# Tile order, shared rounds and filler products in the causal attentions of a four-layer decoder kernel

## Chip, core and metric

The kernel runs on one core of a Trainium2 chip. The metric is the time of one execution on the device in microseconds (us). The engines are TensorE (PE in the rows, its weight loads PEld), VectorE (DVE), ScalarE (ACT), GpSimd (POOL) and SyncE (SP, which issues the transfers).

## What is computed

A decoder of four layers works on x of shape (4, 512, 128). Each layer has an attention, a cross attention and a feed-forward part, each added to x behind a layer norm:

```python
x = x + _L0_attn_ref(_layernorm(x, axis=-1), ...)
x = x + _L0_xattn_ref(_layernorm(x, axis=-1), ctx_1024, ctx_1024, ...)
x = x + _L0_ffn_ref(_layernorm(x, axis=-1), ...)
...
x = x + _L3_ffn_ref(_layernorm(x, axis=-1), ...)
```

Three of the twelve parts are touched. The attention of layer 0 is a gated delta rule with 16 value heads over chunks: for each chunk a lower triangular matrix is inverted by doubling, and a state is carried from chunk to chunk; its output is gated by silu(x W_z). The feed-forward part of layer 0 is a mixture of 16 experts with 4 chosen. The attentions of layers 1 and 2 are causal softmax attentions over 512 positions with 16 heads: scores q k, masked above the diagonal, softmax over the keys, times v.

## The kernel before

The batch of four is a loop of four passes. A pass runs the twelve parts one after the other, each a block of its own in which every engine has its own program and semaphores order them; engines meet at a block's ends. All matrices lie as 128 partitions times 512 positions; NT = 4 tiles of 128 positions.

`causal_attention` serves both causal attentions, so it runs eight times in an execution. The heads are in G = 4 groups of R = 4; a group's four heads sit in the four 32-row strips of TensorE. PSUM has eight banks of 512 columns. Its work comes in two stages.

The score stage finds each query's peak. TensorE walks through `steps`. A step `("scores", g, i)` makes the scores of query tile i of group g against keys 0 to (i + 1) * 128 (four products, L624, and four small ones, L627, which add the mask on the diagonal) into one half of PSUM, banks 0 to 3 or 4 to 7 in turn. VectorE reduces each to the negated maximum (L705). When all tiles of a group are there, VectorE splits the peaks into a coarse and a fine part (L711 to L716). A step `("turn", g, 0)` transposes these (L633) into the half whose turn it is, and ScalarE copies them to `shiftT` (L679). Step n starts when the content of step n - 2, in the same half, is read.

The second stage makes the probabilities by key tile. A unit u is one key tile j of one group. TensorE computes k q for keys j and queries j * 128 to 512 and adds the negated peaks with a two-row product (`shifted`, L646 and L649, banks 0 to 3). ScalarE takes the exponential of all of it (L685) into one of three slots of `prob`, GpSimd zeroes what is above the diagonal (L695), and TensorE multiplies by v and by ones (`mix`, L663), two units later. VectorE takes the reciprocal of the sums and multiplies (L722, L724), after each group in layer 1 and once in layer 2 (`shared`). TensorE's program is shifted(u), then mix(u - 2), and shifted(u) waits for the exponential u - 1.

In `stage_l0_attn` a step n inverts the matrices of four pairs p in L = 6 levels. Each level has a half level (L2208, in the last level L2204), a copy by ScalarE (L2330), and a whole level (L2223 and L2227, in the last level L2218), and VectorE subtracts (L2498, in levels 5 and 6 L2502 and L2505). Between them TensorE places products of the step before (`ks` L2151, `corrected` L2168, `output` L2177, `add` L2187) and of the step to come (`prep` L2118 and L2122, `turn` L2130), each in two halves: pairs FIRST and SECOND. What it places where is the code after `half_level` and after `whole_level`. After the loop come the eight z products (L2560) and the transpositions of the result (L2568). In `experts_stage` TensorE waits, before the first expert, for the routing on VectorE (`gate_ready`).

`m.warm(pe, count, bank)` issues count products 128x512 in bf16 whose result nobody reads (L88). The text calls them fillers.

Of the kernel before, what the change touches and what calls it, by code (L numbers as in the profile page):

```python
# [25 lines left out]
P = 128  # L26
# [198 lines left out]
def experts_stage(m, name, w, E, inter, route, weigh_output):  # L225
# [18 lines left out]
    with ExitStack() as ctx:  # L244
# [23 lines left out]
        with nc.Block(no_gpsimd_drain=True) as block:  # L268
            @block.tensor
            def _(pe):  # L270
# [5 lines left out]
                def spread(g):  # L276
                    if g == 0:
                        if weigh_output:
                            m.warm(pe, 18, 4)
# [284 lines left out]
def causal_attention(m, name, q_of, k_of, head_of, v, ones_of, shared, mixed):  # L564
# [10 lines left out]
    for g in range(G):  # L575
        for i in range(NT):
            steps.append(("scores", g, i))
            if g > 0 and i == 1:
                steps.append(("turn", g - 1, 0))
    steps.append(("turn", G - 1, 0))  # L580
    with ExitStack() as ctx:
# [22 lines left out]
        U = G * NT  # L604
        mix_bank = lambda g: 4 if shared else 4 + 2 * (g % 2)

        def wait_consumed(pe, n):

            kind, g, i = steps[n]
            if kind == "scores":  # L610
                pe.wait_ge(peak_ready, NT * g + i + 1)
            else:
                pe.wait_ge(shiftT_ready, g + 1)

        with nc.Block(no_gpsimd_drain=True) as block:
            @block.tensor
            def _(pe):
                for n, (kind, g, i) in enumerate(steps):
                    base = 4 * (n % 2)
                    if n >= 2:  # L620
                        wait_consumed(pe, n - 2)
                    if kind == "scores":
# [7 lines left out]
                    else:  # L630
                        pe.wait_ge(shift_ready, g + 1)
                        for t in range(NT):
                            ins = pe.transpose(m.psum[:, base, t * P:(t + 1) * P],  # L633
                                               shift[:, g % 2, t, :, :].rearrange("p r w -> p (r w)"), m.ident)
                        ins.then_inc(shift_psum, 1)

                def shifted(u):
                    g, j = divmod(u, NT)
                    if u == 0:
                        for n in (len(steps) - 2, len(steps) - 1):  # L640
                            wait_consumed(pe, n)
# [3 lines left out]
                    for r in range(R):  # L645
                        pe.matmul(m.psum[:, r, 0:T - j * P], k_of(g)[quad(r), j * P:(j + 1) * P],  # L646
                                  q_of(g)[quad(r), j * P:T], start=True, stop=False)
                    for r in range(R):
                        ins = pe.matmul(m.psum[:, r, 0:T - j * P], one_bf[W * r:W * r + 2, :],  # L649
                                        shiftT[W * r:W * r + 2, g, j * P:T], start=False, stop=True)  # L650
                    ins.then_inc(shifted_psum, 1)

                def mix(u):
                    g, j = divmod(u, NT)
                    pe.wait_ge(causal, u + 1)
                    if not shared and j == 0 and g >= 2:
                        pe.wait_ge(mixed_ready, g - 1)
                    first = u == 0 if shared else j == 0
# [2350 lines left out]
```

## Time and profile before

| | us |
|---|---|
| median of three runs (5857.47 to 5858.99) | 5857.73 |
| the profiled execution, its time | 5875.89 |
| the profiled execution, its span | 5874.2 |
| TensorE busy | 4750.1 |
| VectorE busy | 2985.1 |
| ScalarE busy | 1667.1 |
| GpSimd busy | 850.5 |
| mean granted TensorE clock, share of full | 0.861 |

The span goes from the first to the last instruction; the time has 1.7 us more around it. Busy times are sums over the engine's instructions, in which overlapping ones of TensorE count once. [...]

### The profile page before, as it was taken

The page shows a single profiled execution, that of the slowest core. Times are in us where ns is not written, and L with a number is a line of the kernel's source. Part 1 is how long each engine was busy: PE and PEld are TensorE (multiplying, and loading weights), DVE is VectorE, ACT ScalarE, POOL GpSimd, SP SyncE. Part 2 cuts the span into 40 slices and gives each one's busy share as a digit, 9 for nine tenths or more (in the row PEclk, how much of TensorE's full clock was granted, in tenths as well). Part 3 has the DMA queues.
Part 4 walks back from the last instruction along what each step waited for, and adds up shares of the span by engine and source line. Part 5 has one row for each costly group of instructions (what it writes and reads, how often), then busy time and mean ns, then how long its engine had stood idle before and what let it go on. Part 6 is the DMA issues. An engine that isn't in the chain of part 4 may idle for free. (4 is left out here: it accounts for less than half of the span.)

```text
span 5874.2 us, 96445 instructions
## 1 busy us (share of the span) xinstructions
PE 4750.1 (81%) x37780; PEld 2864.2 (49%) x37780; DVE 2985.1 (51%) x6690; ACT 1667.1 (28%) x3752; POOL 850.5 (14%) x1344
## 2 busy tenths in 40 slices
PE   6988788778798878877879887887787988788778
PEld 4863343445486334344458533434444863343444
DVE  5654534543666444454366644445446654544543
ACT  3431212232343121233134312122323431212331
POOL 1420000210241000021023100002102410000210
PEclk7888898889698989888969888988896988898889
DMA  1000000000000000000000000000000000000000
GB/s 63 3 10 38 15 12 1 18 14 35 21 3 9 38 15 12 1 18 29 24 17 3 9 38 15 12 1 18 9 40 21 3 9 38 15 12 1 18 28 22
DMA packets 11009, 104.26 MB, mean 18 GB/s; under 512 B 1148, under 2 KB 5552, under 8 KB 6192
## 3 DMA queue, kind: packets, MB, share of 16 engines
q1 hardware_dynamic: 10544, 97.91, 4.3%
q8 instruction: 310, 5.08, 0.4%
q14 instruction: 155, 1.27, 0.1%
HBM read 96.86 MB, written 1.05 MB: 17 GB/s over the span
## 5 line engine op out<-in xcount | busy, mean ns | idle before, releaser
L88 PE MATMUL psum<-ident_bf 128*128 128x512 bf16 x1576 | 440.1, 435 | 158.2 <-DVE l_xattn_prob L517 46.9
L88 PEld LDWEIGHTS psum<-ident_bf 128*128 128x128 bf16 x1576 | 158.4, 108 | 428.9 <-issue 163.3
L2498 DVE TENSOR_TENSOR l_attn_xx<-l_attn_xx,psum 128x256 f32<-128x256 f32 x512 | 207.8, 419 | 228.9 <-PE psum L2227 216.2
L375 DVE TENSOR_TENSOR l_ffn_hidden<-l_ffn_silu,psum 128x512 f32<-128x512 f32 (+2 forms) x184 | 126.2, 686 | 331.5 <-ACT l_ffn_silu L332 331.5
L94 PEld LDWEIGHTS psum<-streamed_weights,l_ffn_hidden 128*128 128x128 f32 (+2 forms) x1728 | 231.7, 196 | 117.8 <-issue 104.7
L332 ACT ACTIVATE l_ffn_silu<-psum 128x512 f32<-128x512 f32 (+2 forms) x216 | 128.8, 596 | 563.4 <-PE psum L302 563.3
L2223 PE MATMUL psum<-l_attn_ax,l_attn_xx 64*64 64x64 f32 x5120 | 277.7, 230 | 12.2 <-ACT l_attn_ax L2330 12.2
L2227 PE MATMUL psum<-l_attn_xx,l_attn_ax 64*64 64x64 f32 x5120 | 267.2, 225 | 0.0
L2330 ACT ACTIVATE l_attn_ax<-psum 128x128 f32<-128x128 f32 (+1 forms) x768 | 182.5, 278 | 293.4 <-PE psum L2208 258.1
L722 DVE RECIPROCAL l_attn_inverse<-psum 128x512 f32<-128x512 f32 x20 | 67.1, 3357 | 356.2 <-PE psum L663 356.2
L2396 POOL TENSOR_TENSOR l_attn_part<-l_attn_ab,streamed_weights 128x128 f32<-128x128 f32 x640 | 244.4, 415 | 18.6 <-PE psum L2208 18.6
L94 PE MATMUL psum<-streamed_weights,l_ffn_hidden 128*128 128x128 f32 (+2 forms) x1728 | 235.4, 280 | 9.6 <-DVE l_ffn_hidden L372 5.0
L705 DVE TENSOR_REDUCE l_attn_peak<-psum 128x4 f32<-128x512 f32 (+3 forms) x128 | 189.3, 1488 | 103.6 <-PE psum L627 103.2
L2223 PEld LDWEIGHTS psum<-l_attn_ax,l_attn_xx 64*64 64x64 f32 x5120 | 217.1, 144 | 32.5 <-ACT l_attn_ax L2330 15.0
L186 POOL TENSOR_TENSOR residual<-residual,w_columns 128x512 f32<-128x512 f32 x20 | 21.8, 1091 | 1432.2 <-DVE xn L203 1432.2
L2208 PE MATMUL psum<-l_attn_xx,l_attn_part 64*64 64x64 f32 x5120 | 219.0, 240 | 8.7 <-POOL l_attn_part L2396 6.0
L685 ACT ACTIVATE l_attn_prob<-psum 128x2048 f32<-128x2048 f32 (+3 forms) x128 | 158.3, 1237 | 204.2 <-PE psum L649 204.2
L2227 PEld LDWEIGHTS psum<-l_attn_xx,l_attn_ax 64*64 64x64 f32 x5120 | 215.3, 142 | 0.0
L2208 PEld LDWEIGHTS psum<-l_attn_xx,l_attn_part 64*64 64x64 f32 x5120 | 197.4, 151 | 30.5 <-issue 17.1
L1524 PE MATMUL psum<-l_ffn_qg,l_ffn_state_mid 128*128 128x128 f32 x480 | 92.6, 359 | 142.2 <-DVE l_ffn_gk_log L1701 142.2
L624 PE MATMUL psum<-l_attn_k,l_attn_q 32*128 32x128 f32 (+3 forms) x1024 | 147.7, 656 | 70.4 <-DVE l_attn_peak L705 49.9
L646 PE MATMUL psum<-l_attn_q,l_attn_k 32*128 32x512 f32 (+3 forms) x1024 | 126.1, 567 | 80.6 <-ACT l_attn_prob L685 74.7
(485 smaller groups left out, 9932.6 us busy)
## 6 DMA issues: line engine op xcount, KB each, us to landing
streamed_weights<-pack_l_ffn SPq DMA_DIRECT2D x4, 5412.0 KB, 15.7
streamed_weights<-pack_l_ffn SPq DMA_DIRECT2D x4, 3972.0 KB, 13.3
streamed_weights<-pack_l_attn SPq DMA_DIRECT2D x5, 2848.5 KB, 9.9
streamed_weights<-pack_l_xattn SPq DMA_DIRECT2D x4, 2496.0 KB, 9.3
streamed_weights<-pack_l_ffn SPq DMA_DIRECT2D x4, 2192.0 KB, 8.5
streamed_weights<-pack_l_xattn SPq DMA_DIRECT2D x4, 2048.0 KB, 8.0
streamed_weights<-pack_l_ffn SPq DMA_DIRECT2D x4, 1667.5 KB, 6.6
streamed_weights<-pack_l_attn SPq DMA_DIRECT2D x4, 1107.5 KB, 5.0
```

Source lines behind the costliest of these rows:

```text
L88: pe.matmul(self.bank(bank), self.ident_bf[:, :], self.ident_bf[:, :].unsqueeze(1).to_broadcast([P, NT, P]), start=True, stop=True)
L94: ins = pe.matmul(self.psum[:, OUT, t * P:(t + 1) * P], features[:, t * P:(t + 1) * P], weight, start=first and t == 0, stop=last, skip_gr ...
L332: act.activation(silu[0:r, n % 2, :], m.bank(n % 2)[0:r], ACT.Silu).then_inc(silu_ready, 1)
L624: pe.matmul(m.psum[:, base + r, 0:(i + 1) * P], q_of(g)[quad(r), i * P:(i + 1) * P], k_of(g)[quad(r), 0:(i + 1) * P], start=True, stop=False)
L685: act.activation(prob[:, u % SLOTS, :, 0:T - j * P], m.psum[:, 0:R, 0:T - j * P], ACT.Exp).then_inc(exps_ready, 1)
L705: dve.tensor_reduce(peak[:, g, i, :], m.psum[:, base:base + R, 0:(i + 1) * P], AX, ALU.max, negate=True).then_inc(peak_ready, 1)
L2208: ins = pe.matmul(m.psum[b, p, W * i:W * i + W], part[b, (M * n + l - 1) % 2, p, i, :], xx[b, n % 2, p, X, i, :], start=True, stop=True)
L2223: pe.matmul(m.psum[b, p, P + W * i:P + W * i + W], xx[b, n % 2, p, XT, i, :], ax[b, p, i, :], start=True, stop=True)
L2227: ins = pe.matmul(m.psum[b, p, 256 + W * i:256 + W * i + W], ax[b, p, i, :], xx[b, n % 2, p, XT, i, :], start=True, stop=True)
L2330: act.activation(ax[b, p, :, :], m.psum[b, p, 0:P].rearrange("p (i t) -> p i t", i=2), ACT.Copy).then_inc(ax_ready, 1)
L2396: pool.tensor_tensor(part[:, q % 2, p, :, :], ab[:, n % 2, p, :, 0:W], over_block(w["levels"][:, l, :]), ALU.mult).then_inc(part_ready, 1)
L2498: dve.tensor_tensor(both, both, m.psum[:, p, P:384], ALU.subtract).then_inc(x_less, 1)
```

## The change

In the score stage the four query tiles of a group come widest first, and the turning of group g - 1 behind the second tile. Eight fillers stand ahead of the first tile, three ahead of each group's widest and one ahead of every other step. The last turning leaves `steps`: it is issued behind the first `shifted`, into bank 4, and its copy behind the first exponential. In the second stage key tiles 1 and 3, 384 and 128 queries wide, share one unit of 512 columns, so a group has three units where it had four. Fillers are added in two other places, and in the first layer's attention three of the placed pieces move.

```diff
-                            m.warm(pe, 18, 4)
+                            m.warm(pe, 26, 4)
                         pe.wait_ge(gate_ready, 1)
...
-        for i in range(NT):
+        for i in reversed(range(NT)):
             steps.append(("scores", g, i))
-            if g > 0 and i == 1:
+            if g > 0 and i == 2:
                 steps.append(("turn", g - 1, 0))
-    steps.append(("turn", G - 1, 0))
+    parts = [[(0, 0)], [(1, 0), (3, 3 * P)], [(2, 0)]]
+    units = [(g, part) for g in range(G) for part in parts]
...
+                m.warm(pe, 8, 0)
                 for n, (kind, g, i) in enumerate(steps):
                     base = 4 * (n % 2)
                     if n >= 2:
                         wait_consumed(pe, n - 2)
+                        m.warm(pe, 3 if i == NT - 1 else 1, base)
...
                 def shifted(u):
-                    g, j = divmod(u, NT)
+                    g, part = units[u]
                     if u == 0:
-                        for n in (len(steps) - 2, len(steps) - 1):
-                            wait_consumed(pe, n)
+                        wait_consumed(pe, len(steps) - 1)
+                        m.warm(pe, 3, 0)
                         pe.wait_ge(cleared, 2)
                     else:
                         pe.wait_ge(exps_ready, u)
-                    for r in range(R):
-                        pe.matmul(m.psum[:, r, 0:T - j * P], k_of(g)[quad(r), j * P:(j + 1) * P],
...
+                    for j, c in part:
+                        for r in range(R):
+                            pe.matmul(m.psum[:, r, c:c + T - j * P], k_of(g)[quad(r), j * P:(j + 1) * P],
+                                      q_of(g)[quad(r), j * P:T], start=True, stop=False)
...
                 def mix(u):
-                    g, j = divmod(u, NT)
-                    pe.wait_ge(causal, u + 1)
+                    g, part = units[u]
+                    pe.wait_ge(causal, diagonals[u])
+                    if u == 0:
+                        pe.wait_ge(shiftT_ready, G)
...
                 for u in range(U + 2):
                     if u < U:
                         shifted(u)
+                    if u == 0:
+                        wait_consumed(pe, len(steps) - 2)
+                        turn(G - 1, 4)
                     if u >= 2:
                         mix(u - 2)
...
-                    act.activation(prob[:, u % SLOTS, :, 0:T - j * P], m.psum[:, 0:R, 0:T - j * P],
+                    act.activation(prob[:, u % SLOTS, :, 0:used(part)], m.psum[:, 0:R, 0:used(part)],
                                    ACT.Exp).then_inc(exps_ready, 1)
+                    if u == 0:
+                        act.wait_ge(shift_psum, G)
+                        act.activation(shiftT[:, G - 1, :], m.bank(4), ACT.Copy).then_inc(shiftT_ready, 1)
...
                         elif l == 4:
                             past(n, add, FIRST)
                             coming(n, prep, SECOND)
-                        elif l == 6:
-                            past(n, output, SECOND)
-                            coming(n, turn, SECOND)
+                        elif l == 5:
+                            past(n, corrected, SECOND)
                         if n < STEPS:
                             whole_level(n, l)
...
                         elif l == 5:
-                            past(n, corrected, SECOND)
+                            past(n, output, SECOND)
                         elif l == 6:
+                            coming(n, turn, SECOND)
                             past(n, add, SECOND)
...
                 for n in range(2 * NT):
                     t, half = divmod(n, 2)
+                    if n == 4:
+                        m.warm(pe, 24, 4)
                     if n >= 2:
                         pe.wait_ge(z_ready, n - 1)
```

GpSimd masks the diagonal of each key tile of a unit, so twice in a shared one; VectorE and the semaphores count in the new order. The line numbers of the kernel after are some 6 to 22 higher from here on.

TensorE, score stage of layer 1, the second group of heads and the start of the third, before (L624 a tile's scores, L627 its mask, L633 the turning):

```order
L624 MATMUL psum<-l_attn_k,l_attn_q 128x128 x4
L627 MATMUL psum<-later_bf,ident_bf 128x128 x4
L624 MATMUL psum<-l_attn_k,l_attn_q 128x256 x4
L627 MATMUL psum<-later_bf,ident_bf 128x128 x4
L633 MATMUL psum<-w_const,l_attn_shift 128x128 x4
L624 MATMUL psum<-l_attn_k,l_attn_q 128x384 x4
L627 MATMUL psum<-later_bf,ident_bf 128x128 x4
L624 MATMUL psum<-l_attn_k,l_attn_q 128x512 x4
L627 MATMUL psum<-later_bf,ident_bf 128x128 x4
```

The same group after, where the scores are L639, the mask L642, the turning L627 and the fillers L88:

```order
L88 MATMUL psum<-ident_bf 128x512 x3
L639 MATMUL psum<-l_attn_k,l_attn_q 128x512 x4
L642 MATMUL psum<-later_bf,ident_bf 128x128 x4
L88 MATMUL psum<-ident_bf 128x512
L639 MATMUL psum<-l_attn_k,l_attn_q 128x384 x4
L642 MATMUL psum<-later_bf,ident_bf 128x128 x4
L88 MATMUL psum<-ident_bf 128x512
L627 MATMUL psum<-w_const,l_attn_shift 128x128 x4
L88 MATMUL psum<-ident_bf 128x512
L639 MATMUL psum<-l_attn_k,l_attn_q 128x256 x4
L642 MATMUL psum<-later_bf,ident_bf 128x128 x4
```

The widest tile has moved from the end of a group to its start, and every step has one or three fillers ahead of it.

ScalarE, from the copies of the turned peaks to the second group's first exponential, before:

```order
L679 ACTIVATE l_attn_shiftT<-psum 128x512 x4
L685 ACT_TABLE_LOAD
L685 ACTIVATE l_attn_prob<-psum 128x2048
L685 ACTIVATE l_attn_prob<-psum 128x4x384
L685 ACTIVATE l_attn_prob<-psum 128x4x256
L685 ACTIVATE l_attn_prob<-psum 128x4x128
L685 ACTIVATE l_attn_prob<-psum 128x2048
```

And after, where the exponentials are L700 and the last copy is L704:

```order
L695 ACTIVATE l_attn_shiftT<-psum 128x512 x3
L700 ACT_TABLE_LOAD
L700 ACTIVATE l_attn_prob<-psum 128x2048
L704 ACTIVATE l_attn_shiftT<-psum 128x512
L700 ACTIVATE l_attn_prob<-psum 128x2048
L700 ACTIVATE l_attn_prob<-psum 128x4x256
L700 ACTIVATE l_attn_prob<-psum 128x2048 x2
```

One of the four copies has moved behind the first exponential, and a group has three exponentials where it had four.

TensorE, the first layer's attention, one step from half level 5 to half level 1 of the next step, before (the whole level's four pairs of rows cut to the last):

```order
L2208 MATMUL psum<-l_attn_xx,l_attn_part 64x64 x16
...
L2227 MATMUL psum<-l_attn_xx,l_attn_ax 64x64 x4
L2168 MATMUL psum<-l_attn_r,l_attn_solved 128x64 x4
L2204 MATMUL psum<-l_attn_xx,l_attn_ab 64x64 x8
L2177 MATMUL psum<-l_attn_u,l_attn_pm 128x64 x4
L2130 MATMUL psum<-streamed_weights,l_attn_part 64x64 x8
L2218 MATMUL psum<-l_attn_solved,l_attn_ax 64x64 x8
L2187 MATMUL psum<-l_attn_u_end,l_attn_k 64x128 x2
L2208 MATMUL psum<-l_attn_xx,l_attn_part 64x64 x16
```

The same stretch after, all lines 19 higher:

```order
L2227 MATMUL psum<-l_attn_xx,l_attn_part 64x64 x16
L2187 MATMUL psum<-l_attn_r,l_attn_solved 128x64 x4
...
L2246 MATMUL psum<-l_attn_xx,l_attn_ax 64x64 x4
L2196 MATMUL psum<-l_attn_u,l_attn_pm 128x64 x4
L2223 MATMUL psum<-l_attn_xx,l_attn_ab 64x64 x8
L2237 MATMUL psum<-l_attn_solved,l_attn_ax 64x64 x8
L2149 MATMUL psum<-streamed_weights,l_attn_part 64x64 x8
L2206 MATMUL psum<-l_attn_u_end,l_attn_k 64x128 x2
L2227 MATMUL psum<-l_attn_xx,l_attn_part 64x64 x16
```

The correction stands ahead of whole level 5, the output ahead of half level 6, and the turning behind whole level 6.

## Rows read from the trace of the kernel before

**Rows 1.** The page, its first line: span and instructions

```profile
span 5874.2 us, 96445 instructions
```

**Rows 2.** Windows of attention stages: us, busy of each engine, PEclk, DMA share, GB/s

```profile
589.40:623.80 34.40, 25.39 (x204) 11.99 (x204) 24.63 (x25) 1.79 (x3) 1.09 (x2) 0.80 0.01 2
623.80:628.80 5.00, 3.60 (x16) 1.45 (x16) 0.44 (x4) 1.88 (x2) 0.00 (x0) 0.53 0.00 0
628.80:673.40 44.60, 35.17 (x436) 13.42 (x436) 12.17 (x7) 19.79 (x16) 10.15 (x16) 0.90 0.00 1
2332.10:2370.30 38.20, 29.86 (x204) 13.87 (x200) 24.82 (x25) 1.79 (x3) 0.72 (x2) 0.63 0.00 0
3848.50:3898.60 50.10, 40.73 (x436) 14.72 (x436) 0.00 (x0) 19.79 (x16) 10.15 (x16) 0.78 0.00 1
```

**Rows 3.** Timeline, score stage: start, length, engine, line, operation, [idle <-releaser]

```profile
607.42 1.11 PE L633 MATMUL psum<-w_const,l_attn_shift 128*128 128x128 f32 x4
...
610.79 1.14 PE L624 MATMUL psum<-l_attn_k,l_attn_q 32*128 32x512 f32 x8
610.90 3.96 DVE L705 TENSOR_REDUCE l_attn_peak<-psum 128x4 f32<-128x1536 f32 x2 [2.09 <-PE psum L627]
...
611.87 0.40 PE L627 MATMUL psum<-later_bf,ident_bf 128*128 128x128 bf16 x4
...
614.91 0.71 PE L624 MATMUL psum<-l_attn_k,l_attn_q 32*128 32x256 f32 x8 [1.36 <-DVE l_attn_peak L705]
...
615.27 1.95 DVE L705 TENSOR_REDUCE l_attn_peak<-psum 128x4 f32<-128x512 f32 x2
```

**Rows 4.** Timeline, last reduction to first exponential

```profile
621.52 2.29 DVE L705 TENSOR_REDUCE l_attn_peak<-psum 128x4 f32<-128x2048 f32 x1 [0.25 <-PE psum L627]
...
626.28 2.09 PE L646 MATMUL psum<-l_attn_q,l_attn_k 32*128 32x512 f32 x8 [0.73 <-issue]
...
628.84 1.88 ACT L685 ACTIVATE l_attn_prob<-psum 128x2048 f32<-128x2048 f32 x1 [1.36 <-PE psum L649]
```

**Rows 5.** Timeline, one group of exponentials

```profile
652.35 1.88 ACT L685 ACTIVATE l_attn_prob<-psum 128x2048 f32<-128x2048 f32 x1 [2.12 <-PE psum L649]
...
655.41 1.45 ACT L685 ACTIVATE l_attn_prob<-psum 128x1536 f32<-128x1536 f32 x1 [1.19 <-PE psum L649]
...
657.67 1.07 PE L663 MATMUL psum<-l_attn_prob,l_attn_v 128*32 128x512 f32 x8
657.78 1.02 ACT L685 ACTIVATE l_attn_prob<-psum 128x1024 f32<-128x1024 f32 x1 [0.92 <-PE psum L649]
...
660.13 0.60 ACT L685 ACTIVATE l_attn_prob<-psum 128x512 f32<-128x512 f32 x1 [1.32 <-PE psum L649]
...
662.84 1.88 ACT L685 ACTIVATE l_attn_prob<-psum 128x2048 f32<-128x2048 f32 x1 [2.12 <-PE psum L649]
```

**Rows 6.** Timeline, last group: PE end, first reciprocal

```profile
671.82 0.61 PE L663 MATMUL psum<-l_attn_prob,l_attn_v 128*32 128x256 f32 x8
...
673.37 3.36 DVE L722 RECIPROCAL l_attn_inverse<-psum 128x512 f32<-128x512 f32 x1 [2.79 <-PE psum L663]
```

**Rows 7.** Timeline of PE, first layer's attention, one step

```profile
237.63 0.45 PE L2223 MATMUL psum<-l_attn_ax,l_attn_xx 64*64 64x64 f32 x8 [0.61 <-ACT l_attn_ax L2330]
...
239.64 1.10 PE L2168 MATMUL psum<-l_attn_r,l_attn_solved 128*128 128x64 f32 x8
...
244.54 0.27 PE L2130 MATMUL psum<-streamed_weights,l_attn_part 64*64 64x64 f32 x2 [0.94 <-DVE l_attn_part L2429]
...
246.57 1.97 PE L2208 MATMUL psum<-l_attn_xx,l_attn_part 64*64 64x64 f32 x32
```

**Rows 8.** The same rows some 12 us later

```profile
258.44 1.14 PE L2208 MATMUL psum<-l_attn_xx,l_attn_part 64*64 64x64 f32 x32
```

**Rows 9.** Timeline of PE, z products of the same attention

```profile
396.29 3.78 PE L2560 MATMUL psum<-streamed_weights,xnT 128*128 128x512 f32 x4 [7.75 <-ACT l_attn_z L2581]
```

**Rows 10.** Timeline of PE, first layer's experts

```profile
494.45 4.06 PE L88 MATMUL psum<-ident_bf 128*128 128x512 bf16 x18
502.67 1.02 PE L282 MATMUL psum<-w_const,l_ffn_gate 128*16 128x128 f32 x4 [4.16 <-DVE l_ffn_gate L399]
```

More of the change, by code:

```diff
@@ L617, in _, with turn @@
             def _(pe):
+                def turn(g, bank):
+                    pe.wait_ge(shift_ready, g + 1)
+                    for t in range(NT):
+                        ins = pe.transpose(m.psum[:, bank, t * P:(t + 1) * P],
+                                           shift[:, g % 2, t, :, :].rearrange("p r w -> p (r w)"), m.ident)
+                    ins.then_inc(shift_psum, 1)
+                m.warm(pe, 8, 0)
                 for n, (kind, g, i) in enumerate(steps):
@@ L651, in shifted @@
                     ins.then_inc(shifted_psum, 1)
                 def mix(u):
-                    g, j = divmod(u, NT)
-                    pe.wait_ge(causal, u + 1)
-                    if not shared and j == 0 and g >= 2:
-                        pe.wait_ge(mixed_ready, g - 1)
-                    first = u == 0 if shared else j == 0
-                    last = u == U - 1 if shared else j == NT - 1
-                    for n in range(2):
-                        for r in range(R):
-                            lhsT = v[:, j, head_of(g, r), :] if n == 0 else ones_of(g)
-                            ins = pe.matmul(m.psum[quad(r), mix_bank(g) + n, j * P:T], lhsT,
-                                            prob[:, u % SLOTS, r, 0:T - j * P], start=first, stop=last,
-                                            skip_group_check=True)
+                    g, part = units[u]
@@ new lines, in mix @@
+                    pe.wait_ge(causal, diagonals[u])
+                    if u == 0:
+                        pe.wait_ge(shiftT_ready, G)
+                    if not shared and u % len(parts) == 0 and g >= 2:
+                        pe.wait_ge(mixed_ready, g - 1)
+                    for j, c in part:
+                        for n in range(2):
+                            for r in range(R):
+                                lhsT = v[:, j, head_of(g, r), :] if n == 0 else ones_of(g)
+                                ins = pe.matmul(m.psum[quad(r), mix_bank(g) + n, j * P:T], lhsT,
+                                                prob[:, u % SLOTS, r, c:c + T - j * P],
+                                                start=j == 0 and (g == 0 or not shared), stop=True, skip_group_check=True)
@@ L679, in _ @@
                         act.activation(shiftT[:, g, :], m.bank(4 * (n % 2)), ACT.Copy).then_inc(shiftT_ready, 1)
-                for u in range(U):
-                    j = u % NT
+                for u, (g, part) in enumerate(units):
                     act.wait_ge(shifted_psum, u + 1)
```

35 lines of the change are left out of this document (17 added, 18 removed).

## The prediction

> **What bounds the kernel now.** I read the page's first line for the span [rows 1], then windows over the stages of the eight causal attentions (layers 1 and 2, four passes each), then the timeline inside one of them, then the places of the first layer that the diff touches. [...]
>
> In the windows [rows 2] an attention has two stages. Its score stage took 34.4 us at a mean clock of 0.80 in one attention and 38.2 at 0.63 in another; its exponentials 44.6 at 0.90 and 50.1 at 0.78. Between the two lie 5.0 us: the last reduction ends at 621.52 + 2.29 = 623.81 and the first exponential starts at 628.84 [rows 4]. Low clock has a price here: a mean of 0.80 is 40% of the time at half speed, so 13.8 us of 34.4, and 0.63 is 28.3 us of 38.2; 3.8 us longer for 14.5 us more of it is 0.26 us for each us at the low level. The exponentials give (50.1 - 44.6)/(22.0 - 8.9) = 0.42. I use 0.3.
>
> In the score stage VectorE's reductions are the heavy side: 3.96 + 1.95 = 5.91 us for the four tiles of a group [rows 3]. One group is 8.6 us (606.68 to 615.27 by the reductions' starts). The rest is waiting: the reduction at 610.90 sat idle for 2.09 us. The turning (L633) takes one of the two PSUM halves, so the next score tile can't be made while a reduction runs.
>
> In the exponentials ScalarE and TensorE take turns [rows 5]. One group runs from 652.35 to 662.84, 10.49 us: 1.88 + 1.45 + 1.02 + 0.60 = 4.95 of exponentials and 1.19 + 0.92 + 1.32 + 2.12 = 5.55 of waits for TensorE.
>
> **The change, part by part.** I work at the high level first, and add the low clock afterwards.
>
> *Score stage.* A group still has 5.91 us of reductions and 0.38 between the last of them and the next group's first (615.27 less the end at 614.89 of the two before it). Wide tiles come first now, and fillers (128x512 products that nobody reads, 4.06/18 = about 0.22 us each [rows 10]) stand ahead of each tile but not in its shadow. The 512 wide tile waits for the 256 wide one's reduction; then come three fillers, 0.65, and the tile with its mask, 611.87 + 0.40 - 610.79 = 1.48 [rows 3], 2.15 with the handover. The 128 wide reduction and the 0.38 cover 1.06 of it: 1.1 idle. The 256 wide tile still waits for the 384 wide one's reduction, because the turning has the other half: one filler and about 1.04 of tile, 1.3 idle. A group costs 5.91 + 0.38 + 1.1 + 1.3 = 8.7. The first group has no turning but eight fillers and the widest tile before any reduction: 1.7 + 1.5. Sum: 3.2 + 4 x 5.91 + 3 x (0.38 + 1.1 + 1.3) = 35.2 us. The old order by the same sums is about 31 at the high level (a first tile of 0.9, 4 x 5.91, three groups with 0.4 and one idle stretch of about 1.4, and 1 for the first fill); what was measured is 34.4 to 38.2, since it sat at the low level for 40% to 74% of the time. So fillers buy clock with time. TensorE's pause while the 384 wide tile is reduced stays, so I keep the clock low for a quarter to a third of the stage, 10 us at 0.3: 38.2. Against a middle of 36 before: **+2.3**, with ends of -1 (clock held) and +8 (clock as before, each filler 0.43).
>
> *Handover.* Casts, turning and its copy no longer stand before the first exponential. What stays is three fillers and the products: at the low level 628.84 - 626.28 = 2.56 [rows 4], at the high one about 1.4. That makes 2.1 to 3.9; I take 2.8 against 5.0: **-2.2**. The last turning runs under the first exponential, its copy (0.60) under the products of the second round.
>
> *Exponentials.* The 384 and 128 wide tiles share one of 1.88 instead of 1.45 + 0.60: 0.17 less. Its products are both tiles': the gap is 1.19 and the 128 wide tile's share. That share is 0.6: the products of L663 at 657.67, two halves of 1.07 with 0.2 in common, run 0.7 past the exponential's end at 658.80, and the gap was 1.32. The gap before the 256 wide one stays 0.92, the one before the next group 2.12 (L663 of the 512 wide tile again outlasts the exponential before it). Group: 1.88 + 1.79 + 1.88 + 0.92 + 1.02 + 2.12 = 9.6 against 10.49. POOL's mask is two of 0.6 us for the shared round, and its reader comes two rounds later: hidden. The end is longer: before, 10.53 from the last group's first exponential to the reciprocal (662.84 to 673.37); now 6.5 to the last exponential's start, then L663 for 512, 512 and 256 columns, 1.9 + 2.0 + 0.9 (671.82 shows 0.61 for half of the last, so 0.9 with both [rows 6]), 11.2. Sum 3 x 9.6 + 11.2 = 40.0. The first group has no L663 in its first two rounds, and I give it 4 us of low clock, 1 us: 41. Before, 44.6 in the quiet case and 50.1 in the other, 46 as a middle: **-5.0**, ends -3.6 and -9.
>
> One attention: 2.3 - 2.2 - 5.0 = -4.9. Eight: **-39 us**.
>
> *First layer's attention.* In level 5 TensorE idled 0.61 before L2223, and in level 6 0.94 at the turning L2130 [rows 7]. The correction L2168, 1.10 us, now comes ahead of L2223; it waits for the qs copies and fills the first hole, but ends some 0.3 us later than L2223 began. VectorE's chain behind L2223 (the x reductions, then prep, then the part that L2130 waits for) so slips by 0.3. L2218 has moved ahead of L2130 and uses the second hole, so 1 us of work is out of the way after it. What is late next is POOL's part chain, which starts after prep and slips by the same 0.3. The gain is 0 to 0.3 a step; 32 steps, I take 0.1: **-3**. The clock matters more here: the 32 products of L2208 took 1.97 us just after the hole and 1.14 in a dense stretch [rows 7, 8]. One low stretch more or less in each step is about 1.5 us, so bounds of -48 and +48 on this part, both far from likely.
>
> [...]
>
> *z products.* 24 fillers, 5.2 us, stand before the fifth product. Its reader comes after the idle 7.75 us [rows 9], so they are hidden, and leave 2.5 us of pause. The two products after the pause took 3.78 at the low level and would take 1.9. With an even chance of it, **-1.2** a pass, bounds 0 and -2: **-5**.
>
> *Experts.* 8 more fillers in a pause of 4.16 [rows 10] leave 2.4, so they are hidden. The products after it ran low. The gate's turning and copy make another pause just behind, so mostly the clock still falls: **-2** a pass, bounds 0 and -7: **-8**.
>
> Sum: -39 - 3 - 5 - 8 = -55 us, on the profiled execution's 5875.9, which gives 5821. The median of the runs lies 18.2 lower, and I carry the difference over whole: 5857.7 - 55 = 5803.
>
> **The rivals.**
> 1. *The clock holds.* Fillers keep TensorE at the high level through whole attentions: 35.2 + 2.1 + 40.0 = 77.3 against 87, -9.7 each, -78, with the experts at -28 and z at -8: 5741. For it: every stage above has its low stretches next to pauses. Against: the pauses in the score stage stay, one before the turning and one behind it. Half of this (5770) is likelier than all. Chance 0.16.
> 2. *Attentions pay for their fillers.* The score stage keeps its low share of 40% to 74%, fillers cost 0.43 there, and the stage goes to 44: +8 each. With -2 and -4.5, +1.5 each, +12 in all, and with 0.3 a step lost in the first layer (+10) and nothing gained elsewhere: 5880, slower. It decides from a score stage above 36 + 6.7 = 43 us. Against: at a filled low level TensorE is all but full, and dense stretches in these rows run high. Chance 0.09.
> 3. *The moved order shifts the low stretches of the first layer* against its steps. A quarter of the bound is 12 us, half is 24: with the worse sign half of it gives 5827, all of it 5851, no change. Chance of all or near it 0.08; of the good sign, 5755 to 5780, 0.07.
> 4. *The change doesn't do what it says*: score stage and exponentials cancel at about the same clocks as now, 5850 to 5865: 0.08.
>
> The forecast itself has 0.52, with its own range of 5780 to 5828.
>
> **How the numbers follow.** The difference of 0.2% is 11.7 us, and about what a measurement of this kernel can tell: below 5846 is faster, above 5869.4 slower. Rivals 1 and the good side of 3, and the forecast, are faster; of rival 3's bad side and of rival 4 a part. That gives faster 0.82, same 0.10, slower 0.08. The range leaves out the upper end of rivals 2 and 4 and the lower half of rival 1: 5762 to 5848. It is made wide by the clock, not by the relay sums.
>
> **What would show it.** In the profile after: score stages of 36 to 40 us with the reduction idle in two places of a group; 2 to 4 us from the last reduction to the first exponential; groups of 9.6 us between exponentials 512 wide, three to a group, with gaps near 1.8, 0.9 and 2.1; 11 us for the last. Steps of the first layer's attention within 0.3 us of now. Wrong would be score stages above 43, groups of exponentials above 10.5, a last turning that delays the second exponential, or a step of the first layer that differs by over 1 us.

## The result, and the profile after

The changed kernel took 5776.38 us (median of 4 runs, 5764.32 to 5778.37); the kernel before took 5857.6 beside it (4 runs, 5848.02 to 5858.99). The ratio is 0.9854, 95% interval 0.9835 to 0.9873, wholly below 1: faster, though by less than 2%. On a second chip (5 and 11 runs) the two took 5766.32 and 5875.88 us, ratio 0.9801 (0.978 to 0.9823). The intervals don't meet, so the gain is 81 us in one comparison and 110 in the other; most of the difference is the kernel before, whose medians lay between 5857.6 and 5876.13 us in four comparisons. The forecast was -55, to 5803. 5776 lies within its range of 5762 to 5848, but 4 us below the likeliest case's own range of 5780 to 5828, in the 5755 to 5780 that was given to the good side of rival 3.

The page's first line and its clock row, to hold against [rows 1]; the span is 98 us shorter than that of the profiled execution before, which was itself 18 us above its median:

```profile
span 5775.9 us, 97157 instructions
...
PEclk7989899889689989988969998997896999899889
```

Windows over a layer 1 attention (score stage, handover, exponentials) and over a layer 2 attention (the same), pass 0 and pass 1, to hold against [rows 2]. Columns: stretch, length, busy PE, PEld, DVE, ACT, POOL, granted clock, DMA share, GB/s. The clock is a share of TensorE's full one; its records in the trace hold two values, 1.00 and 0.50, which the text calls the high and the low level:

```profile
581.50:618.70 37.20, 28.78 (x235) 12.97 (x235) 24.53 (x25) 3.08 (x4) 1.08 (x2) 0.95 0.01 2
618.70:620.90 2.20, 2.17 (x16) 0.77 (x17) 0.44 (x3) 0.02 (x1) 0.00 (x0) 1.00 0.01 4
620.90:661.90 41.00, 34.37 (x440) 14.25 (x440) 12.15 (x6) 19.60 (x13) 9.98 (x16) 0.92 0.00 1
2308.80:2347.40 38.60, 30.00 (x236) 12.87 (x236) 24.45 (x26) 3.08 (x4) 1.07 (x2) 0.93 0.00 1
2347.40:2349.60 2.20, 2.20 (x16) 0.79 (x17) 0.41 (x3) 0.05 (x1) 0.00 (x0) 1.00 0.00 0
2349.60:2389.70 40.10, 33.39 (x440) 13.76 (x439) 0.04 (x1) 19.57 (x13) 9.97 (x16) 0.96 0.01 2
```

The two score stages take 37.2 and 38.6 us where the same two took 34.4 and 38.2 before, although their clock is 0.95 and 0.93 instead of 0.80 and 0.63; handover and exponentials are shorter. Taken with the same edges over all eight attentions (POOL's clearing of the shift tile, the end of the last reduction, the first exponential, the last reciprocal), the means in us are:

| mean of eight | before | after | change |
|---|---|---|---|
| score stage | 36.0 | 38.1 | +2.1 |
| handover | 5.0 | 2.6 | -2.5 |
| exponentials | 46.1 | 40.5 | -5.6 |

Timeline of the score stage of that first attention, one group, to hold against [rows 3]:

```profile
598.95 0.82 PE L88 MATMUL psum<-ident_bf 128*128 128x512 bf16 x3 [0.34 <-DVE l_attn_peak L724]
...
601.21 3.96 DVE L724 TENSOR_REDUCE l_attn_peak<-psum 128x4 f32<-128x2048 f32 x2 [1.21 <-PE psum L642]
...
603.56 0.39 PE L88 MATMUL psum<-ident_bf 128*128 128x512 bf16 x1 [0.98 <-DVE l_attn_peak L724]
603.78 0.60 PE L627 MATMUL psum<-w_const,l_attn_shift 128*128 128x128 f32 x4
...
605.22 0.39 PE L88 MATMUL psum<-ident_bf 128*128 128x512 bf16 x1 [0.84 <-DVE l_attn_peak L724]
605.54 0.71 PE L639 MATMUL psum<-l_attn_k,l_attn_q 32*128 32x256 f32 x8
...
606.62 1.82 DVE L724 TENSOR_REDUCE l_attn_peak<-psum 128x4 f32<-128x1024 f32 x2 [1.46 <-PE psum L642]
```

The reductions wait in the two places the prediction named: 1.21 us at the 512 wide tile (1.1 forecast) and 1.46 at the 256 wide one (1.3). In both a filler (L88) starts only when the wait is over, so it stands on the path.

The exponentials of a middle group, to hold against [rows 5]:

```profile
651.34 1.88 ACT L700 ACTIVATE l_attn_prob<-psum 128x2048 f32<-128x2048 f32 x1 [2.12 <-PE psum L661]
...
654.68 1.88 ACT L700 ACTIVATE l_attn_prob<-psum 128x2048 f32<-128x2048 f32 x1 [1.47 <-PE psum L661]
...
657.48 1.03 ACT L700 ACTIVATE l_attn_prob<-psum 128x1024 f32<-128x1024 f32 x1 [0.92 <-PE psum L661]
```

Three rounds and three gaps: 1.88 + 1.47 + 1.88 + 0.92 + 1.03 + 2.12 = 9.30 us, against 10.49 before.

The first layer moved more than the forecast had it. Windows of two consecutive steps of its attention, before (pass 0) and after (the same two steps in pass 2):

```profile
195.16:226.52 31.36, 30.33 (x610) 26.85 (x609) 19.55 (x64) 14.61 (x57) 12.90 (x28) 0.89 0.01 3
226.52:259.71 33.19, 31.55 (x618) 27.75 (x617) 21.16 (x72) 15.10 (x61) 12.89 (x28) 0.90 0.01 3
```

```profile
3079.82:3109.63 29.81, 28.45 (x610) 25.06 (x609) 19.28 (x65) 14.62 (x57) 12.91 (x28) 1.00 0.01 3
3109.63:3140.35 30.72, 29.22 (x618) 25.61 (x617) 20.88 (x72) 15.07 (x61) 12.91 (x28) 1.00 0.01 3
```

The same instructions in another order, nearly the same busy time on the other engines, and a clock of 1.00 instead of 0.89 and 0.90. Before has such a quiet step in none of its four passes. Of the experts [rows 10], after shows:

```profile
501.26 0.60 PE L282 MATMUL psum<-w_const,l_ffn_gate 128*16 128x128 f32 x4 [0.79 <-DVE l_ffn_gate L399]
```

The pause ahead of L282 is 0.79 us, not 4.16, and the four products take 0.60 us at a granted clock of 1.00 (501.2 to 501.9 us), against 1.02 us at 0.50 before (502.0 to 503.7 us).

Added up between the residual additions, over four passes and in the profiled executions, the -98 us are: first layer's attention with z -26, its experts -16, the attention parts of layers 1 and 2 with their projections -42, the cross attention behind layer 2's attention -13 (in each pass 77.9 us before and 74.7 after), the rest -2 (rounded, so they add up to 99).

### The profile page after: what moved, and what is told of

Same layout as the page of the kernel before. It is cut to its first block and busy times, and to the rows that moved or that the text cites. A ratio compares the mean times of both kernels' runs of the same rounds, so it can differ in the third digit from the quotient of the medians.

```text
span 5775.9 us, 97157 instructions
## 1 busy us (share of the span) xinstructions
PE 4717.3 (82%) x38180; PEld 2851.8 (49%) x38180; DVE 2979.8 (52%) x6690; ACT 1658.7 (29%) x3720; POOL 849.7 (15%) x1344
## 5 line engine op out<-in xcount | busy, mean ns | idle before, releaser
L88 PE MATMUL psum<-ident_bf 128*128 128x512 bf16 x1976 | 555.0, 425 | 247.6 <-DVE l_attn_peak L724 67.2
L88 PEld LDWEIGHTS psum<-ident_bf 128*128 128x128 bf16 x1976 | 195.7, 106 | 566.9 <-issue 194.1
L724 DVE TENSOR_REDUCE l_attn_peak<-psum 128x4 f32<-128x2048 f32 (+3 forms) x128 | 185.5, 1487 | 121.7 <-PE psum L642 120.8
L700 ACT ACTIVATE l_attn_prob<-psum 128x2048 f32<-128x2048 f32 (+1 forms) x96 | 153.0, 1594 | 180.5 <-PE psum L661 180.5
L301 PE MATMUL psum<-l_ffn_gated_x,streamed_weights 128*128 128x512 f32 (+1 forms) x320 | 169.4, 611 | 0.0
L302 PE MATMUL psum<-l_ffn_gated_x,streamed_weights 128*128 128x512 f32 (+1 forms) x320 | 163.4, 592 | 0.0
```

What stands on the lines that cost most here:

```text
L88: pe.matmul(self.bank(bank), self.ident_bf[:, :], self.ident_bf[:, :].unsqueeze(1).to_broadcast([P, NT, P]), start=True, stop=True)
L301: pe.matmul(m.bank(n % 2)[0:r], w["up"][:, c:c + r], rhs, start=True, stop=True)
L302: pe.matmul(m.bank(2 + n % 2)[0:r], w["gate"][:, c:c + r], rhs, start=True, stop=True).then_inc(up_ready, 1)
L700: act.activation(prob[:, u % SLOTS, :, 0:used(part)], m.psum[:, 0:R, 0:used(part)], ACT.Exp).then_inc(exps_ready, 1)
L724: dve.tensor_reduce(peak[:, g, i, :], m.psum[:, base:base + R, 0:(i + 1) * P], AX, ALU.max, negate=True).then_inc(peak_ready, 1)
```

## The experiments

Each is timed beside the kernel before. The product of the first three ratios below is 0.9788; together they measured 0.9801 in c0_after, so by that comparison the parts add up. By the first comparison (0.9835 to 0.9873) they don't, and in the traces the experts are 12 us shorter with the order alone, 18 with the fillers alone and 16 to 17 with both.

| kernel | median us | ratio (95%) |
|---|---|---|
| a1_attn: attentions alone | 5809.41 | 0.9886 (0.9863 to 0.991) |
| a2_order: first layer's order alone | 5845.82 | 0.9949 (0.9929 to 0.997) |
| a3_fill: z and experts alone | 5847.44 | 0.9951 (0.9932 to 0.9971) |
| a4_attn_bare: attentions without fillers | 5791.89 | 0.9859 (0.9836 to 0.9883) |
| c0_after: the whole change | 5766.32 | 0.9801 (0.978 to 0.9823) |
| c1_best, e0_best: the change without the attentions' fillers | 5752.9, 5754.85 | 0.9793 (0.9772 to 0.9814), 0.9798 (0.9778 to 0.9818) |
| c2_lead: with the eight leading ones | 5770.0 | 0.9805 (0.9784 to 0.9827) |
| c3_corr: a third of the order | 5906.59 | 1.0057 (1.0037 to 1.0078) |
| d1_corr_out: two thirds of the order | 5891.49 | 1.0035 (1.0015 to 1.0055) |
| d2_units: the shared round alone | 5836.01 | 0.9941 (0.9922 to 0.9959) |
| e1_shadow: fillers under a wait | 5719.42 | 0.9739 (0.9719 to 0.9759) |

**The three parts by themselves.** a1_attn is before with the new `causal_attention`, a2_order is before with this part of the diff alone, a3_fill has the other two fillers:

```diff
 # a2_order                              # a3_fill
-elif l == 6:                            -m.warm(pe, 18, 4)
-    past(n, output, SECOND)             +m.warm(pe, 26, 4)
-    coming(n, turn, SECOND)             ...
+elif l == 5:                            +if n == 4:
+    past(n, corrected, SECOND)          +    m.warm(pe, 24, 4)
```

> The kernel before with the changed causal attention alone; the first layer's order and the fillers of z and of the experts are as before. In the two traces an attention took 91.2 us before and 85.2 after, mean of eight. Theory: those 6 us are the attention's own (fewer and better covered waits, and its fillers), and a quieter stage behind it gives 0 to 3 us a pass more, so the time falls by 45 to 60 us, to 5798 to 5813. Rival 1: part of the 6 us is clock that the other edits set up ahead of the attention; then under 40 us are gained here. Rival 2: the whole -81 us is the attention's work, the other parts being worth nothing: 5777.

> The kernel before with the moved order of the first layer's attention alone (the correction products, the outputs and the turning half a level or a level elsewhere). The theory on record is -3 us, 5855, with steps within 0.3 us. Rival 1: the traces' -26 us of the first layer's attention (-1, 0, -14, -11 us in the four passes) is the order's, by fewer low stretches in two passes: 5832. Rival 2: the order alone loses, since the correction ends later than the first x product began: 0.3 us a step, +10, 5867.

> The kernel before with the fillers of the z products (24 a pass) and of the experts (8 more a pass) alone. On record: -5 for z and -8 for the experts, so -13, 5845. Rival 1: the traces' -16 us in the first layer's feed-forward part is all due to these eight fillers, and with z's -5 it gives -21, 5837. Rival 2: a pause behind each makes the clock fall anyway, and nothing is gained: within 3 us of 5858.

The attentions gave 1.14%, 67 us of 5876.13, a little more than the theory. Order (0.51%, 30 us) and fillers (0.49%, 29 us) gave nearly as much together as the attentions did, and in both a rival was nearer than the forecast: the order's 30 us is rival 1's. Its trace shows the same quiet steps as after, so the order is enough for them, without the changed attentions and fillers:

```profile
3103.31:3133.12 29.81, 28.43 (x610) 25.06 (x609) 19.27 (x65) 14.55 (x57) 12.89 (x28) 1.00 0.01 3
3133.12:3163.84 30.72, 29.22 (x618) 25.62 (x617) 20.90 (x73) 15.02 (x61) 12.89 (x28) 1.00 0.01 3
```

In a3_fill's trace the stage from the last step's start to the residual addition, z included, is 2.3 us shorter in each pass (-9 in all), and the experts -7.1, +2.7, -7.1 and -6.4 (-18). The +2.7 falls in the pass that was already quick before (58.2 us against 61.5); there the clock still fell, for 13.7 us of 61.0.

**Fillers in the attention.** a4_attn_bare is a1_attn, c1_best is the changed kernel, both with

```diff
-                m.warm(pe, 8, 0)
-                        m.warm(pe, 3 if i == NT - 1 else 1, base)
-                        m.warm(pe, 3, 0)
```

and c2_lead puts the first of the three lines back.

> The kernel before with the changed causal attention but without any of that attention's fillers (the 8 ahead of the first tile, the 3 or 1 ahead of each tile and the 3 ahead of the first shifted tile). Theory: order, shared round and moved turning give the handover's 2.5 us and the exponentials' 4 to 5; the score stage without fillers saves their 3 us but runs at the low level for half of its time again, +13 us low at 0.3 = +4, so it ends 1 us longer than with them: an attention of 86 us, -40 us for the eight, 5818. Rival 1: the fillers' clock is the gain: an attention of 89 to 91 us and 5840 to 5858. Rival 2: the fillers cost more than their clock gives: 82 to 84 us, 5785 to 5800, faster than with them.

> The changed kernel itself, on the chip of the three runs beside it. The parts alone measured 0.9886 (attentions), 0.9949 (order) and 0.9951 (fillers of z and experts). Theory: they are worth the same together, 0.9788 by their product, but the pair was measured as 0.9854 against another set of runs of before, so I expect 0.980 to 0.986. Rival: they share one gain of the clock, and the ratio stays above 0.986.

> The changed kernel without the fillers inside its causal attentions; the moved order of the first layer and the fillers of z and of the experts stay. Theory: alone, those attention fillers cost 17 us (0.9886 with them, 0.9859 without; an attention of 85.7 us against 82.1), and nothing else depends on them: the changed kernel's time less 10 to 25 us, about 5758. Rival: they keep the clock of later stages (the cross attention of layer 2 gained 11 to 13 us with them, 7 without), so the difference is under 5 us.

> As the run before it, with the eight products ahead of an attention's first tile kept. Theory: without any filler the score stage took 31.8 us at 4 us of low level in layer 1, and 36.3 at 22.6 us in layer 2; eight fillers delay each first tile by 1.7 us, so layer 1 loses 1.7, and layer 2 gains up to 4.4 - 1.7 where they keep the clock: between +14 and -4 us over the eight. Rival: layer 2's clock falls later in the stage whatever stands ahead of it, and the eight cost their full +14 us.

Without its fillers an attention (the three stages of the table and the last reciprocal and product, 4.1 us more) took 82.1 us in a4_attn_bare and 83.8 in c1_best, against 85.7 in a1_attn and 85.6 in c0_after; before it was 91.2. Windows over a layer 1 and a layer 2 score stage of a4_attn_bare:

```profile
591.00:622.85 31.85, 21.36 (x204) 10.42 (x204) 24.41 (x25) 3.07 (x4) 1.09 (x2) 0.94 0.01 2
869.30:905.50 36.20, 29.23 (x204) 13.19 (x204) 24.68 (x25) 3.07 (x4) 1.05 (x2) 0.69 0.00 1
```

At nearly the clock of after's first attention (0.94 against 0.95) the stage is 31.85 instead of 37.20: 31 fillers, 6.8 us at 0.22 each, cost 5.35. At a clock of 0.69 it still takes only 36.20. So in the score stage the fillers cost more than they bring, as rival 2 of a4_attn_bare says. Behind the attentions they give some of it back: layer 2's cross attention is 11 us shorter in a1_attn and 7 in a4_attn_bare. In time this is 0.9859 against 0.9886 and, in the whole change, 0.9793 and 0.9798 against 0.9801; the medians differ by 17 and by 11 to 13 us, but the intervals overlap, so that gain isn't settled by these runs. c2_lead is no better than c1_best and not told apart from c0_after: nothing shows a use for the eight leading ones. The handover is 2.6 us in a4_attn_bare and stays at 5.0 in d2_units below, so the shared round has no part in its gain. The moved last turning and the order of the query tiles, widest first, weren't tried apart.

**Which part of the order.** c3_corr moves only the corrections, d1_corr_out the outputs too; the turning stays ahead of level 6's whole products in both.

```diff
 # c3_corr, ahead of whole_level         # d1_corr_out
+elif l == 5:                            +elif l == 5:
+    past(n, corrected, SECOND)          +    past(n, corrected, SECOND)
 elif l == 6:                             elif l == 6:
     past(n, output, SECOND)             -    past(n, output, SECOND)
     coming(n, turn, SECOND)                  coming(n, turn, SECOND)
                                          # behind whole_level
                                         +elif l == 5:
                                         +    past(n, output, SECOND)
```

> The kernel before with one third of the first layer's new order: the correction products of the second pair ahead of level 5's whole products, outputs and turning where they were. Theory: the hole of 0.61 us ahead of those products is what let the clock fall in a step; filled, a step has 0 to 3.4 us of low level instead of 6.8, and the gain is that of the whole order, 0.9949 or about -25 us. Rival 1: the hole ahead of the turning (0.94 us) is the one, and this gives 0 to -5 us. Rival 2: it takes both, and one alone gives about half, -12.

> The kernel before with the correction products and the outputs of the second pair moved as in the change (ahead of and behind level 5's whole products), the turning left ahead of level 6's whole products. The corrections alone made it slower, 1.0057: in that trace the hole had moved on, into level 6's half products (2.53 us from first to last instead of 1.2), and the clock fell behind it. Theory: the outputs, 1.10 us, must stand in that hole; with them the ratio is that of the whole order, 0.995 to 0.997. Rival: the turning, which waits for POOL's part with level 6's whole products queued behind it, is what costs; then it stays at 1.000 to 1.005.

My theory fell twice. Both are slower than before. d1_corr_out came out as its rival, the turning, had it (1.000 to 1.005), and it differs from a2_order in the turning's place alone: with the other two moves there, moving the turning takes the ratio from 1.0035 to 0.9949. Whether the outputs' move brings anything on top of the corrections' isn't told apart (1.0057 and 1.0035, intervals overlap). In c3_corr's trace the hole of level 5 comes back between level 6's half products, in waits of 0.24, 0.37 and 0.37 us. TensorE's timeline of one step in d1_corr_out:

```profile
3163.76 1.10 PE L2177 MATMUL psum<-l_attn_u,l_attn_pm 128*128 128x64 f32 x8
3164.79 1.40 PE L2204 MATMUL psum<-l_attn_xx,l_attn_ab 64*64 64x64 f32 x16
3167.26 0.45 PE L2130 MATMUL psum<-streamed_weights,l_attn_part 64*64 64x64 f32 x8 [1.07 <-DVE l_attn_part L2430]
3168.65 0.37 PE L2130 MATMUL psum<-streamed_weights,l_attn_part 64*64 64x64 f32 x2 [0.94 <-DVE l_attn_part L2430]
...
3169.05 1.59 PE L2218 MATMUL psum<-l_attn_solved,l_attn_ax 64*64 64x64 f32 x13
```

and the same place in after (L2187, L2196, L2223, L2237 and L2149 there are L2168, L2177, L2204, L2218 and L2130 of before):

```profile
3120.25 1.08 PE L2187 MATMUL psum<-l_attn_r,l_attn_solved 128*128 128x64 f32 x8
...
3123.27 1.10 PE L2196 MATMUL psum<-l_attn_u,l_attn_pm 128*128 128x64 f32 x8
3124.31 1.23 PE L2223 MATMUL psum<-l_attn_xx,l_attn_ab 64*64 64x64 f32 x13
...
3125.50 1.01 PE L2237 MATMUL psum<-l_attn_solved,l_attn_ax 64*64 64x64 f32 x13
3126.77 0.45 PE L2149 MATMUL psum<-streamed_weights,l_attn_part 64*64 64x64 f32 x8 [0.26 <-DVE l_attn_part L2448]
3128.16 0.45 PE L2149 MATMUL psum<-streamed_weights,l_attn_part 64*64 64x64 f32 x8 [0.94 <-DVE l_attn_part L2448]
```

In d1_corr_out the turning waits 1.07 + 0.94 us, the whole products L2218 are queued behind it, and they run at the low level (granted clock 0.50, 1.59 us for what takes 1.01). In after the whole products use the first of those waits, and 0.26 + 0.94 are left. So filling the hole at level 5 without moving the turning only pushed it to the turning, where it holds up more work; the step took 33.50 us at 0.90. Of the partial orders tried none gains, all three moves together do. The moved turning without the other two wasn't tried.

**The shared round alone.** d2_units is before with `units` and `parts` of the diff; score order, turnings and handover are before's.

```diff
+    parts = [[(0, 0)], [(1, 0), (3, 3 * P)], [(2, 0)]]
+    units = [(g, part) for g in range(G) for part in parts]
-                for u in range(U):
+                for u, (g, part) in enumerate(units):
```

> The kernel before with one third of the new attention: two key tiles share a round of the exponentials (three rounds a group instead of four); score stage, turnings and handover as before, no fillers. Theory: it gives the groups of exponentials of 9.3 us instead of 10.5, so three times 1.2 us and 0.5 at the end, -4 us an attention, -32, ratio 0.9945; the handover stays at 5 us. Rival: what the round saves comes from its quicker clock behind the fillers; then the groups stay above 10 us and the ratio is above 0.998.

0.9941 against the 0.9945 expected. Its exponentials' window in the first attention, to hold against the third of [rows 2] (44.60 at 0.90):

```profile
629.00:671.40 42.40, 35.19 (x436) 14.52 (x436) 12.15 (x6) 19.11 (x12) 9.96 (x16) 0.85 0.01 2
```

2.2 us shorter at a lower clock; groups are 9.3 us without any filler, and the mean of eight is 42.1 against 46.1. In time the shared round is half of what the attentions gain (0.59% of 1.14%). Here as in after the middle groups are 9.3 us and the last is 10.6; what is left of the difference to after's 40.5 lies in the first group, with 10 to 13 us of low level here and 3.4 to 6.8 there.

**Fillers where they cost nothing.** e1_shadow is c1_best with three products behind each turning, ahead of the wait that L637 has anyway. They write banks of the turning's half that nobody reads.

```diff
                         turn(g, base)
+                        m.warm(pe, 3, base + 1)
```

> The changed kernel without its attention fillers once more, beside the next one. Theory as before: 0.979 to 0.980, 5745 to 5760.

> As the run before it, and three products 512 columns wide behind each turning, in the banks of its half that nobody reads, ahead of the wait for the 384 wide tile's reduction. That wait was 1.01 us long in the trace without fillers, and three are 0.65 at the high level. Theory: fillers under a wait cost nothing and keep the clock: the score stage falls from 35.3 (18.6 low) to about 33, -10 to -20 us in all. Rival 1: the pause of 1.2 us ahead of the turning lets the clock fall anyway: within 5 us. Rival 2: at the low level three are 1.3 us, more than the wait, and the stage grows: +5 to +10 us.

35 us faster than the kernel without them, where 10 to 20 were expected, and the fastest of all: 5719.42 us, ratio 0.9739, clearly below the change's 0.9801. Windows over the same two score stages, and the timeline behind a turning:

```profile
581.20:613.00 31.80, 23.42 (x213) 11.04 (x213) 24.29 (x25) 3.07 (x4) 1.07 (x2) 0.95 0.00 1
855.70:889.20 33.50, 27.01 (x213) 12.49 (x213) 24.50 (x25) 3.07 (x4) 1.09 (x2) 0.82 0.00 1
```

```profile
600.60 0.66 PE L627 MATMUL psum<-w_const,l_attn_shift 128*128 128x128 f32 x4 [1.20 <-DVE l_attn_peak L722]
601.09 0.81 PE L88 MATMUL psum<-ident_bf 128*128 128x512 bf16 x3
...
602.26 0.71 PE L637 MATMUL psum<-l_attn_k,l_attn_q 32*128 32x256 f32 x8 [0.36 <-DVE l_attn_peak L722]
...
603.34 1.82 DVE L722 TENSOR_REDUCE l_attn_peak<-psum 128x4 f32<-128x1024 f32 x2 [1.14 <-PE psum L640]
```

L637 still has 0.36 us to wait behind the three, so they cost nothing. Nine of them in a score stage hold the clock of layer 1 as 31 on the path did (0.95), and that of layer 2 in part: 0.82, against 0.93 with the 31 and 0.69 without any. The pause of 1.20 ahead of the turning didn't spoil it (rival 1). An attention is 79.4 us: score stage 32.7 against 35.7 in e0_best, handover 1.46 against 2.47, exponentials 41.1 against 41.6. 4.5 us times eight is 36.

## Why the prediction was right, and where it wasn't

**Score stage, handover, exponentials** (+2.3, -2.2, -5.0): measured +2.1, -2.5 and -5.6. Both idle places, the 9.6 us group (9.30) and the last group (10.6 for 11.2) were where the relay sums, in which TensorE and VectorE or ScalarE wait for each other in turn, had them. Part of the agreement is luck. One score stage of a1_attn ran at the high level throughout and took 35.9 us, 0.7 more than the sum; after's had 5.5 us of low level on average instead of 10, but each cost 0.39 (38.1 - 35.9 over 5.5) instead of 0.3. And the exponentials' first group took 10.9 to 11.9 us where the sum had 10.6, which took back more than half of what the other three were shorter. The one estimate that was off is the share of the 128 wide tile in the shared round's gap, 0.6; the gap is 1.47, so the share is 0.28. An attention changed by -6.0 us, forecast -4.9: -48 instead of -39.

**"Fillers buy clock with time"** held, and a4_attn_bare shows on which side the trade comes out: they cost 5.35 us on the path, and the clock returns less. Rival 2 (the attentions pay for their fillers) was right that they are paid for and wrong about the size: the stage never came near 43 us. Rival 1 (the clock holds) came half true: 0.92 to 0.96 in the windows above, but with the fillers paid for.

The sum takes each filler as paid in full where VectorE already waits for the tile behind it. The traces show most of that: in after's score stage the filler starts at 603.56 and the turning behind it at 603.78, the next filler at 605.22 and its tile at 605.54; 31 fillers ahead of the tiles that VectorE waits for cost 5.35 of 6.8 us, and three products ahead of a wait left 0.36 us of it.

**The first layer's order** (-3) is the step that failed. The relay part was right: the turning starts 0.5 us later in a step, since VectorE's chain slips (0.3 forecast), and at equal clock a step changes little: in pass 1 the seven steps from the first half product to that of the last step took 218.9 us with 41.5 us of low level before and 218.3 with 40.8 after, 0.1 us a step. What was wrong is the size of the clock's part. I put "one low stretch more or less in each step" into the bounds, called them far from likely, and gave the good sign of rival 3 a chance of 0.07. Measured alone, the order is 30 us, and a step of 33.19 us becomes 30.72 with its clock at 1.00. The step's pauses on TensorE went from 0.61 + 0.94 us [rows 7] to 0.26 + 0.94, and with them some steps stayed at the high level throughout: of the 28 such steps in four passes none before, nine in a2_order, five in after. A row was at hand: the 0.83 us by which L2208 is slower behind the hole [rows 7, 8] in a stretch that nearly every step had, were too large to carry as noise around zero when the change uses that very hole.

**z** (-5) gave -9, beyond its bound of -2 a pass, and **the experts** (-8) gave -18 in a3_fill. For the experts the step that failed is "mostly the clock still falls": in a3_fill it fell for 3.4 to 6.8 us instead of 17.3 in three passes, which reached the bound of -7 or nearly, and in the fourth for 13.7. The pause, too, came out shorter than the 2.4 us of the forecast: in after's first pass the eight fillers took 2.1 us, and the routing was there 1.3 us earlier.

**Left out of the sum** was what stands behind the changed stages. Layer 2's cross attention has no changed line, and each pass of it is 3.2 us shorter (clock 0.96 instead of 0.92), 13 us in all, 11 of them in a1_attn too; with the order alone the experts, whose own code is untouched there, took 12 us less. The stage doesn't start at a better clock: its first 2.0 us (before) and 3.2 us (after) in pass 0 run at the low level. But before has two more low stretches, 8.8 to 12.2 and 15.6 to 19.0 us into it, and after has none until its end. What decides where such a stretch falls isn't settled here.

The sum of -55 was short by 26 us in one comparison and 55 in the other, and these items all err to the same side: each effect of the clock was entered well below its bound. Against 5857.7 the range of 5762 to 5848 is -96 to -10 us: the first comparison's 81 lies in it, the second's 110 doesn't, so that the range held is in part luck.

## What to carry to other kernels

Fillers that keep TensorE's clock belong ahead of a wait, in banks that nobody reads, not behind it: nine under a wait gave 35 us, 31 on the path lengthened their stage by more than the clock gave back in it. In a relay, don't put a waiting instruction ahead of ready work of the same queue: with the turning ahead of the whole products TensorE waited 1.07 + 0.94 us in a step, behind them 0.26 + 0.94. A hole that is filled in one place can come back as a longer one a level later (0.61 us in before, 0.24 + 0.37 + 0.37 in c3_corr), so measure a reordering as a whole and in parts. And where a change fills a pause ahead of a stretch that runs at the low level in every step, forecast the clock's part at its likely size, and look at the stages behind it, whose low stretches can move as well: layer 2's cross attention went from 77.9 to 74.7 us with no line of it changed.

## What the runs showed of the hardware

The records of the granted clock hold two values, 1.00 and 0.50 of full, in all 14 traces: before's have 211 stretches of each, and their mean over its span is 0.861. In before and after a filler starts 0.216 us after the one ahead of it at 1.00 and 0.427 us at 0.50 (medians of fillers that follow each other).

The granted clock falls in stretches in which TensorE is busy for most of the time. In before's step of 33.19 us PE counts 31.55 us as busy, its timeline shows two pauses, 0.61 and 0.94 us, and the clock is 0.90. A step of after shows 0.26 and 0.94 us, and its clock is 1.00 in pass 2 but 0.90 in the last step of pass 0 (32.60 us), with the same two pauses. So the pauses alone don't decide it; what else does isn't settled. The same code can meet a different clock in each pass: after's experts took 54.4, 55.1, 56.1 and 61.0 us.

One us at the low level cost (218.3 - 211.3) / (40.8 - 10.9) = 0.23 us in the first layer's attention (seven steps of passes 1 and 2 of after). In the experts, 61.5 us at 17.3 us of low level before and 54.4 at 3.4 in after, it cost 0.51. In the score stage it cost (35.68 - 32.67) / (20.8 - 7.9) = 0.23 between e0_best and e1_shadow, and (38.3 - 35.9) / 7.0 = 0.34 between two passes of a1_attn.
